# First products of a stage made in the pauses of the stage ahead, at five seams, and one expert split beside the ternary layer

## The chip, the cores and the metric

The kernel runs on one core of one Trainium2 chip. The metric is the device time of one execution in microseconds, median of several runs; lower is better. The core has a matrix engine (TensorE, PE), a vector engine (VectorE, DVE), a scalar engine (ScalarE, ACT), GpSimd (POOL) and a synchronising engine (SyncE, SP) that issues most transfers. TensorE writes into PSUM, which has eight banks.

## The reference

Two blocks, each an attention followed by a feed-forward part, every part with a residual and a layer norm. Input: 2 x 1024 rows of 512.

```
x = layernorm(x + L0_attn(x))   # q, k, v products, rope, causal softmax, 32 query heads on 8 key heads, wo
x = layernorm(x + L0_ffn(x))    # layer norm, absmax rounding, ternary w_fc (512 -> 2048), exact gelu,
                                # layer norm, absmax rounding, ternary w_proj (2048 -> 512)
x = layernorm(x + L1_attn(x))   # features elu(x Wqk + b), silu(x Wv + b), silu(x Wu + b); kv = k^T v;
                                # out = layernorm(q kv) * u; out Wo + b    (16 heads of 32, linear attention)
x = layernorm(x + L1_ffn(x))    # 16 routed experts (512 -> 2 x 352 -> 512, top 2) and a shared one twice as wide
```

The experts' weights come as 32-bit floats. A product of 32-bit accuracy is made from half-precision parts: each operand is split into a high and a low half, and high x high, high x low and low x high are added up (12 matmuls for a 128 x 512 result over 512 columns).

## The kernel before

The rows are worked in tiles of 128. The program is a row of stages, each a `Phase` with its own buffers, semaphores and PSUM banks and a block in which each engine has its own instruction list; between two stages all engines meet at a barrier. The stages, by the span's time: layer 0 of the attention (0 to 346, first batch) and layer 1 (346 to 666, second batch), both by `attention_layer`; `ternary_ffn` (to 907); `linear_features` ("lin", the feature stage, to 1099); `linear_output_and_route` ("out", to 1211); `dispatch` ("disp", to 1318.5); the routed experts; the shared half and the sum. The order within an engine's list is written out by hand: `unrolled` takes a table of (delay, function) pairs and calls, step by step, each function for the tile that is due; the attention's order comes from a planner that the change doesn't touch.

*The attention's two layers.* A tile is turned (`transpose_parts`, L164), multiplied with q, k and v weights (`products`, L156, 12 matmuls each), rotated on VectorE (L772, L777) and GpSimd (L892), and turned again (L550). At the end of a layer each of eight row tiles has its ending: VectorE normalises, ScalarE (L730) and GpSimd (L942) make the halves, TensorE turns them (event "x") and multiplies with wo (event "w", L156); VectorE adds and normalises (L868, L209, L226). Layer 1 also prepares two "early rows" for the ternary layer: `early_rows` on VectorE, `early_root` on GpSimd.

*The ternary layer.* Per tile 32 matmuls `fc` (L1084, four banks), gelu on ScalarE (L1106), mean and spread, normalisation (ScalarE L1138), maximum (VectorE L990), clip (L996), high half (ScalarE L1133), low half (VectorE L1194), a transpose by DMA into `hT`, 32 matmuls `proj` (L1094), residual (L1199) and norm. Between the normalisation and the next maximum one row block of the feature stage's weights is split (`next_high` L1144, `next_low` L1210).

*The feature stage.* Per tile three banks of `weighed` (L1337, 12 matmuls each) with a `biased` matmul each (L1341), exponential and tanh on ScalarE (L1434, L1439), VectorE (L1485 and on), then `kv` (L1411, L1417). Beside it `ExpertSplit` works on the weights of 14 experts, seven pieces each, 98 in all: load (SyncE), high half (ScalarE L1312), low half (VectorE L1317), store, in a ring of six; `spread` gives each tile's step its share of them.

*Output and routing, dispatch.* `q` (L1602) multiplies features with kv; near the end a tile is turned (L164), ScalarE evacuates it (L1671), `logit` follows (L1631). `dispatch` begins with `SharedHalf.gate_up` (24 matmuls of 128 x 352 a tile, L156), turns (L1782) and `down` (L1791), with the routing's sums and scatters between.

## Time and profile before

| | us |
|---|---|
| runs (3), lowest, median, highest | 1738.38, 1739.52, 1745.71 |
| profiled execution, its own time | 1740.19 |
| its span | 1738.4 |
| TensorE busy | 1585.8 (91%) |
| VectorE busy | 1176.6 (68%) |
| ScalarE busy | 933.9 (54%) |
| GpSimd busy | 576.3 (33%) |
| mean granted clock of TensorE | 0.973 |

The span runs from the first to the last instruction. Busy times of engines overlap. The granted clock is a share of 2.4 GHz: 0.5 is the lower level, 1.2 GHz, and a value between them is a mean over a stretch with both. Matmuls are pipelined, so a group's busy time counts and not the sum of single ones.

### The profile page before, as it was taken

How to read it: one execution, taken by the hardware profiler on the slowest of the kernel's cores; microseconds unless marked ns; L12 is line 12 of the kernel's file. 1: busy time of each engine (PE TensorE's matmuls, PEld its weight loads, DVE VectorE, ACT ScalarE, POOL GpSimd, SP SyncE). 2: the span in 40 equal slices, each digit the busy share in tenths (PEclk: the TensorE clock that was granted, in tenths of full speed). 3: DMA queues.
4: the chain of work that ended last, by engine and by line, in shares of the span. 5: the costliest groups of instructions: out<-in, count | busy, mean ns of one | idle time of the engine just before them, and what ended most of it. 6: DMA issues, size and time to landing. Idle time of an engine off the chain costs nothing. (4 is left out here: it accounts for less than half of the span.)

```text
span 1738.4 us, 33564 instructions
## 1 busy us (share of the span) xinstructions
PE 1585.8 (91%) x12554; PEld 803.7 (46%) x12554; DVE 1176.6 (68%) x2074; ACT 933.9 (54%) x1641; POOL 576.3 (33%) x583
## 2 busy tenths in 40 slices
PE   6899999889999997999978999687898899999997
PEld 3533333364333342444434444454555556666564
DVE  4599998468999955899857777895723243333387
ACT  5756777345677754767736665476223333333332
POOL 4556575161000021223321111595271111111265
PEclk9999999899999998999999999798999999999999
DMA  7323332000000002655638999551151764456344
GB/s 248 137 39 56 76 68 48 2 1 2 14 2 2 2 2 63 125 109 110 106 73 315 353 334 363 179 182 61 55 101 51 276 226 167 154 179 219 105 126 134
DMA packets 177842, 211.42 MB, mean 122 GB/s; under 512 B 114203, under 2 KB 117625, under 8 KB 175505
## 3 DMA queue, kind: packets, MB, share of 16 engines
q1 hardware_dynamic: 170336, 188.54, 36.3%
q0 software_dynamic: 7344, 20.73, 4.4%
q8 instruction: 101, 1.65, 0.4%
q14 instruction: 61, 0.49, 0.1%
HBM read 193.33 MB, written 56.40 MB: 144 GB/s over the span
## 5 line engine op out<-in xcount | busy, mean ns | idle before, releaser
L717 ACT ACTIVATE layer_scratch<-layer_banks 128x512 f32<-128x512 f32 x576 | 312.5, 596 | 128.7 <-PE layer_banks L609 127.2
L828 DVE TENSOR_REDUCE layer_mx<-layer_banks 128x2 f32<-128x1024 f32 (+3 forms) x304 | 339.2, 1156 | 24.0 <-PE layer_banks L587 20.6
L2218 PE MATMUL sparse_ps_g<-wgate,sparse_xT 128*128 128x352 f16 x1128 | 185.5, 315 | 1.6 <-DVE sparse_xT L2296 1.6
L624 PE MATMUL layer_banks<-layer_scratch,V 128*32 128x256 f32 x2304 | 174.5, 389 | 0.8 <-ACT layer_scratch L725 0.8
L1337 PE MATMUL lin_ps_z<-arena,early 128*128 128x512 f16 x576 | 134.5, 384 | 6.8 <-PEq L1044 3.5
L2218 PEld LDWEIGHTS sparse_ps_g<-wgate,sparse_xT 128*128 128x128 f16 x1128 | 108.9, 98 | 63.1 <-DVE sparse_xT L2296 2.0
L2302 DVE SCALAR_TENSOR_TENSOR sparse_hid<-sparse_th,sparse_ps_g 128x352 f32<-128x352 f32 x47 | 24.5, 521 | 155.8 <-ACT sparse_th L2263 155.8
L2329 POOL DMA_INDIRECT xg<-x_d,token x45 | 42.6, 947 | 252.5 <-PE sparse_ps_x L2208 252.5
L1094 PE MATMUL ffn_ps_y<-wprojT,ffn_hT 128*128 128x512 f16 x512 | 116.1, 386 | 8.0 <-DMA ffn_hT<-ffn_h 8.0
L1084 PE MATMUL ffn_ps_fc<-wfcT,early 128*128 128x512 f16 x512 | 114.7, 383 | 5.7 <-PEq L950 3.4
L587 PE MATMUL layer_banks<-KT,arena 64*128 64x512 f16 (+3 forms) x768 | 113.8, 330 | 6.5 <-DVE layer_mx L828 6.3
L609 PE MATMUL layer_banks<-arena,KT 64*128 64x256 f16 x1152 | 111.9, 273 | 6.1 <-ACT layer_scratch L717 4.3
L2250 PE MATMUL sparse_ps_y<-wdown,sparse_hT 128*128 128x512 f16 (+1 forms) x423 | 100.6, 383 | 10.4 <-ACT sparse_hT L2276 9.1
L1317 DVE SCALAR_TENSOR_TENSOR lin_sp_parts<-lin_sp_raw,lin_sp_parts 128x704 f16<-128x704 f32 (+2 forms) x98 | 78.6, 840 | 36.6 <-ACT lin_sp_parts L1312 36.5
L1312 ACT ACTIVATE lin_sp_parts<-lin_sp_raw 128x704 f16<-128x704 f32 (+2 forms) x98 | 67.3, 718 | 55.8 <-DMA lin_sp_raw<-in_L_ffn_w_gate_up_dram 40.2
L1337 PEld LDWEIGHTS lin_ps_z<-arena,early 128*128 128x128 f16 x576 | 53.6, 99 | 73.2 <-issue 13.5
L220 POOL TENSOR_TENSOR ffn_lnr_rstd<-ffn_lnr_var,minus_half 128x1 f32<-128x1 f32 x16 | 36.7, 2297 | 141.7 <-DVE ffn_lnr_var L215 141.7
L1094 PEld LDWEIGHTS ffn_ps_y<-wprojT,ffn_hT 128*128 128x128 f16 x512 | 50.6, 99 | 71.4 <-DVE ffn_r L1199 5.5
L1084 PEld LDWEIGHTS ffn_ps_fc<-wfcT,early 128*128 128x128 f16 x512 | 50.2, 98 | 68.5 <-issue 6.4
L942 POOL TENSOR_TENSOR layer_turned_rows<-O,layer_turned_rows 128x512 f16<-128x512 f32 x16 | 18.5, 1158 | 186.7 <-ACT layer_turned_rows L730 186.7
L624 PEld LDWEIGHTS layer_banks<-layer_scratch,V 128*32 128x32 f32 x2304 | 49.6, 108 | 63.8 <-issue 35.1
L609 PEld LDWEIGHTS layer_banks<-arena,KT 64*128 64x128 f16 x1152 | 39.0, 94 | 86.1 <-issue 42.0
(305 smaller groups left out, 3129.4 us busy)
## 6 DMA issues: line engine op xcount, KB each, us to landing
wgate<-gate_d SPq DMA_DIRECT2D x47, 1408.0 KB
wdown<-down_d SPq DMA_DIRECT2D x47, 768.0 KB
lin_sp_raw<-in_L_ffn_w_gate_up_dram SPq DMA_DIRECT2D x56, 352.0 KB, 5.0
gate_d<-lin_sp_parts SPq DMA_DIRECT2D x56, 352.0 KB, 4.8
y_d<-y SPq DMA_DIRECT2D x47, 256.0 KB
down_d<-lin_sp_parts SPq DMA_DIRECT2D x42, 256.0 KB, 4.7
lin_sp_raw<-in_L_ffn_w_down_dram SPq DMA_DIRECT2D x28, 256.0 KB, 5.3
wfcT<-in_L_ffn_w_fc_dram SPq DMA_DIRECT2D x8, 512.0 KB, 7.6
```

The source lines that it names most:

```text
L587: last = pe.matmul(slots[par][:, h, :], QT[s, pair + h, qt * P:(qt + 1) * P], KT[s, (pair + h) // 2, c * 512:c * 512 + n], start=not diago ...
L609: last = pe.matmul(ps_t[:, (2 * g + par) % 3, i, :], KT[s, j, kt * P:(kt + 1) * P], QT[s, 2 * j:2 * j + 2, qt * P:(qt + 1) * P], start=kt ...
L624: last = pe.matmul(ps_o[32 * jj:32 * jj + 32, 256 * half:256 * half + 256], V[:, kt, 4 * jg + jj, :], prob[(2 * q + jj // 2) % 4][:, half, ...
L717: act.activation(prob[g % 4][:, par, :, :], ps_t[:, (2 * g + par) % 3, :, :], ACT.Exp, scale=HD ** -0.5).then_inc(exp_done, 1)
L828: dve.tensor_reduce(mx[x % 2][:, c, :, at:at + per], ps_s[:, 2 * (r % 2):2 * (r % 2) + 2, 0:per * n].rearrange("p e (h k) -> p e h k", k=n ...
L1084: last = pe.matmul(ps_fc[n][:, :], xT[u][:, part, k, :], m.wfcT[:, k, n * D:(n + 1) * D], start=(k == 0 and part == 0), stop=(k == KC - 1 ...
L1094: last = pe.matmul(ps_y[u][:, :], hT[u][:, part, k, :], m.wprojT[:, k, :], start=(k == 0 and part == 0), stop=(k == NK - 1 and part == 1))
L1312: act.activation(self.part(i, 0), self.raw[u][0:rows, 0:width], ACT.Copy, scale=WS).then_inc(self.hi_done, 1)
L1317: dve.scalar_tensor_tensor(self.part(i, 1), self.raw[i % self.ring][0:rows, 0:width], WS, self.part(i, 0), ALU.mult, ALU.subtract).then_in ...
L1337: pe.matmul(out, xT[:, a, k, :], m.w1[:, i, b, k, :], start=(k == 0 and n == 0), stop=False)
L2218: last = pe.matmul(ps_g[u][n][rows, :], xT[u][:, a, k, rows], w, start=(k == 0 and i == 0), stop=(k == KC - 1 and i == 2), skip_group_chec ...
L2250: last = pe.matmul(ps_y[u][rows, :], hT[u][0:size, a, k, rows], w, start=(k == 0 and i == 0), stop=(k == 2 and i == 2), skip_group_check=L ...
```

## The change

All stages share one PSUM tensor of eight banks, `m.banks`, so that a result can stay in its bank over a barrier. At five seams the stage ahead makes products of the next stage's first tiles.

- Layer 0 to layer 1: the 12 q matmuls of tile 0 (128 x 512) ahead of the turning of the last tile, the 12 k matmuls (128 x 128) behind the last wo. Layer 1 makes only v for tile 0.
- Layer 1 to the ternary layer: 8 fc matmuls of tile 0 ahead of the last turning, 16 behind the last wo; 8 remain.
- Ternary layer to feature stage: 24 `weighed` matmuls ahead of the last `proj`, 12 behind it; only the three `biased` remain for tile 0.
- Feature stage to output: 18 query matmuls of tiles 0 and 1 ahead of the last `kv`; 6 remain.
- Output to dispatch: 42 gate-up matmuls of tiles 0 and 1 ahead of the last four logits; 6 remain.

In layer 1 `early_rows` takes its statistics a step earlier, its two normalisations in steps 5 and 6 instead of both in step 6, and stands behind `qlo` instead of ahead of `first_maxima`; `early_root` moves a step earlier. One expert's seven pieces move from the feature stage (91 left) to the ternary layer, one in every second step, with a ring of three.

```diff
+        def next_projection(pe, at, size):
+            out = banks[:, 4:6, :].rearrange("p n c -> p (n c)")[:, at:at + size]
+            products(pe, out, lambda k: xT[0][:, 0, k, :], lambda k: xT[0][:, 1, k, :],
+                     lambda k: m.wqkv_h[:, k, at:at + size], lambda k: m.wqkv_l[:, k, at:at + size], KC)
+        def next_layer(pe, n):
+            ternary_products(pe, m, m.banks[:, 4 + n, :], xT[0], n)
...
                 if kind == "x":
                     t, = a
+                    if t == TB - 1:
+                        pe.wait_ge(exp_done, 4 * len(QUADS))
+                        pe.wait_ge(early_in[0], 16)
+                        if ternary:
+                            next_projection(pe, 0, D)
+                        else:
+                            next_layer(pe, 0)
                     pe.wait_ge(ol_done, t + 1)
...
                              lambda k: m.wo_h[:, k, :], lambda k: m.wo_l[:, k, :], KC).then_inc(y_done, 1)
+                    if t == TB - 1 and ternary:
+                        next_projection(pe, D, KV)
+                    elif t == TB - 1:
+                        next_layer(pe, 1)
+                        next_layer(pe, 2)
...
             def early_rows(t, u):
-                    if t == 4:
+                    if t == 3:
                         early_ln.statistics(dve, m.X[:, n, :][:, None, :], n, n)
-                    if t == 6:
+                    if t == 5 + n:
                         early_ln.normalize(dve, early_x[n][:, :], m.X[:, n, :], n, n)
...
                 def proj(t):
+                    if t == NT - 1:
+                        pe.wait_ge(gelu_done, NT * NB)
+                        pe.wait_ge(xt_in[0], 16 * (NT // 2))
+                        pe.wait_ge(w1l_done, NT)
+                        for i in range(2):
+                            weighed(pe, m, m.banks[:, 4 + i, :], i, xT[0])
...
+                    if t == NT - 1:
+                        weighed(pe, m, m.banks[:, 6, :], 2, xT[0])
...
-                                      (4, of_layer(h_norm)), (1, of_layer(next_high))])
+                                      (4, of_layer(h_norm)), (1, of_layer(next_high)),
+                                      (5, split.every_second(split.high, act))])
...
-                                      (1, of_layer(x_norm)), (1, of_layer(next_low))])
+                                      (1, of_layer(x_norm)), (1, of_layer(next_low)), (5, split.every_second(split.low, dve))])
...
-        split = ExpertSplit(f, m, d, 6, 0, LIN_EXPERTS, 0)
+        split = ExpertSplit(f, m, d, 6, FFN_EXPERTS, LIN_EXPERTS - FFN_EXPERTS, 0)
...
                 def kv(t):
+                    if t == NT - 1:
+                        pe.wait_ge(xt_evac, NT - AHEAD)
+                        pe.wait_ge(kvl_done, 4)
+                        for n in range(2):
+                            queries(pe, m, n, range(KC - 1))
                     pe.wait_ge(k_done, t + 1)
...
+                def shared(t):
+                    if t == NT - 4:
+                        pe.wait_ge(split.lo_done, split.count)
+                        pe.wait_ge(n1_done, NT)
+                        shared_gate_up(pe, m, 0, 0, range(KC))
+                    if t == NT - 3:
+                        shared_gate_up(pe, m, 0, 1, range(KC - 1))
+                    if t == NT - 2:
+                        pe.wait_ge(wt_evac, NT)
+                        shared_gate_up(pe, m, 1, 0, range(KC))
+                    if t == NT - 1:
+                        shared_gate_up(pe, m, 1, 1, range(KC - 1))
-                unrolled(NT, [(3, wt), (0, q), (8, xt), (9, logit), (4, wo), (2, router)])
+                unrolled(NT, [(3, wt), (0, q), (8, xt), (9, shared), (9, logit), (4, wo), (2, router)])
```

VectorE in the ternary layer, before: the low half of a weight row block (into `arena`), then the maximum of the gelu rows `ffn_hn` and their clip.

```order
L1210 SCALAR_TENSOR_TENSOR arena<-ffn_raw,arena 128x512
L990 TENSOR_REDUCE ffn_qh_g<-ffn_hn 128x1
L993 TENSOR_SCALAR ffn_qh_limit<-ffn_qh_g 128x1 x2
L996 TENSOR_SCALAR ffn_hn<-ffn_hn,ffn_qh_limit 128x2048
L1177 TENSOR_REDUCE ffn_whole<-ffn_sums 128x1
```

The same place now, in every second tile:

```order
L1264 SCALAR_TENSOR_TENSOR arena<-ffn_raw,arena 128x512
L1372 SCALAR_TENSOR_TENSOR ffn_sp_parts<-ffn_sp_raw,ffn_sp_parts 128x704
L1033 TENSOR_REDUCE ffn_qh_g<-ffn_hn 128x1
L1036 TENSOR_SCALAR ffn_qh_limit<-ffn_qh_g 128x1 x2
L1039 TENSOR_SCALAR ffn_hn<-ffn_hn,ffn_qh_limit 128x2048
```

A piece's low half stands between the weight row block's low half and the maximum.

TensorE at the seam from the ternary layer to the feature stage, before: the last three `proj` in one row (96 matmuls), the two branches at the barrier, then the feature stage's first products.

```order
L1094 MATMUL ffn_ps_y<-wprojT,ffn_hT 128x512 x96
L1044 UNCONDITIONAL_BRANCH
L1379 UNCONDITIONAL_BRANCH
L1337 MATMUL lin_ps_z<-arena,early 128x512 x36
L1341 MATMUL lin_ps_z<-bias,ones_row 128x512 x3
```

And now:

```order
L1145 MATMUL banks<-wprojT,ffn_hT 128x512 x64
L1401 MATMUL banks<-arena,early 128x512 x24
L1145 MATMUL banks<-wprojT,ffn_hT 128x512 x32
L1401 MATMUL banks<-arena,early 128x512 x12
L1088 UNCONDITIONAL_BRANCH
L1452 UNCONDITIONAL_BRANCH
L1405 MATMUL banks<-bias,ones_row 128x512 x3
```

All 36 products stand ahead of the barrier, 24 of them between the last two `proj`.

TensorE at the seam from output to dispatch, before: turning the last tile, two tiles' logits, the barrier, the gate-up products of two tiles.

```order
L164 MATMUL out_ps_x<-ident,out_x 128x128 x8
L1631 MATMUL out_ps_l<-out_gT,xT 128x16 x32
L1571 UNCONDITIONAL_BRANCH
L2077 UNCONDITIONAL_BRANCH
L156 MATMUL disp_ps_g<-arena,xT 128x352 x48
```

And now, from the same turning on:

```order
L170 MATMUL banks<-ident,out_x 128x128 x8
L1840 MATMUL banks<-arena,xT 128x352 x12
L1703 MATMUL banks<-out_gT,xT 128x16 x16
L1840 MATMUL banks<-arena,xT 128x352 x9
L1703 MATMUL banks<-out_gT,xT 128x16 x16
L1647 UNCONDITIONAL_BRANCH
L2173 UNCONDITIONAL_BRANCH
L1840 MATMUL banks<-arena,xT 128x352 x6
```

21 of the 42 products that moved stand here ahead of the last two logits, 21 more ahead of the two logits before.

## Rows read from the trace of the kernel before

**Rows 1.** Windows: span, busy us (count) by engine, PEclk, DMA share, GB/s

```profile
340.00:360.00 20.00, 15.01 (x123) 8.66 (x122) 9.38 (x23) 2.86 (x6) 7.62 (x12) 0.86 0.01 2
...
666.20:906.60 240.40, 226.55 (x1024) 100.81 (x1024) 196.13 (x382) 157.92 (x225) 61.92 (x62) 0.98 0.55 105
...
906.60:1098.70 192.10, 177.70 (x928) 87.33 (x928) 141.38 (x202) 112.01 (x186) 34.22 (x32) 0.96 0.90 324
```

**Rows 2.** Timeline (start, us, engine, operation, [idle before, releaser]), layer 0 end

```profile
335.92 1.04 PE L164 MATMUL layer_banks<-ident,layer_turned_rows 128*128 128x128 f16 x8 [2.77 <-POOL layer_turned_rows L942]
...
337.74 0.61 PE L156 MATMUL layer_banks<-wo_h,layer_turned_rows 128*128 128x512 f16 x1 [0.79 <-DVE layer_turned_rows L864]
...
342.67 0.69 DVE L868 SCALAR_TENSOR_TENSOR layer_r<-layer_banks,X 128x512 f32<-128x512 f32 x1 [4.53 <-PE layer_banks L156]
```

**Rows 3.** Timeline, layer 1's start

```profile
346.03 0.58 PE L156 MATMUL layer_banks<-wqkv_h,early 128*128 128x512 f16 x1 [3.40 <-PEq L950]
...
348.24 0.09 DVE L809 MEMSET layer_top<- 128x16 uint32 x2
...
351.63 0.82 DVE L772 TENSOR_TENSOR layer_scratch<-layer_banks,consts 128x640 f32<-128x640 f32 x1 [3.31 <-PE layer_banks L156]
```

**Rows 4.** Timeline, early rows in layer 1, its end, ternary layer start

```profile
385.42 1.81 PE L550 MATMUL layer_banks<-ident,layer_scratch 128*128 128x128 f16 x24 [2.64 <-DVE layer_scratch L783]
...
663.16 0.69 DVE L868 SCALAR_TENSOR_TENSOR layer_r<-layer_banks,X 128x512 f32<-128x512 f32 x1 [4.88 <-PE layer_banks L156]
...
672.99 1.28 ACT L1106 ACT_TABLE_LOAD   x1
```

**Rows 5.** Timeline, the ternary layer's loop in the middle and near its end

```profile
750.27 2.28 DVE L990 TENSOR_REDUCE ffn_qh_g<-ffn_hn 128x1 f32<-128x2048 f32 x1
...
750.93 7.07 PE L1094 MATMUL ffn_ps_y<-wprojT,ffn_hT 128*128 128x512 f16 x32
...
763.93 2.28 DVE L990 TENSOR_REDUCE ffn_qh_g<-ffn_hn 128x1 f32<-128x2048 f32 x1
...
764.75 1.46 PE L1094 MATMUL ffn_ps_y<-wprojT,ffn_hT 128*128 128x512 f16 x6
...
870.38 2.29 DVE L990 TENSOR_REDUCE ffn_qh_g<-ffn_hn 128x1 f32<-128x2048 f32 x1 [2.90 <-ACT ffn_hn L1138]
...
872.95 1.35 DVE L996 TENSOR_SCALAR ffn_hn<-ffn_hn,ffn_qh_limit 128x2048 f32<-128x2048 f32 x1
...
876.13 1.90 ACT L1133 ACTIVATE ffn_h<-ffn_hn 128x2048 f16<-128x2048 f32 x1
```

**Rows 6.** Timeline, the seam to the feature stage

```profile
894.71 8.75 PE L1094 MATMUL ffn_ps_y<-wprojT,ffn_hT 128*128 128x512 f16 x32 [5.03 <-DMA ffn_hT<-ffn_h]
...
916.86 0.80 PE L1341 MATMUL lin_ps_z<-bias,ones_row 33*128 33x512 f16 x3 [2.01 <-DVE bias L1470]
```

**Rows 7.** Feature stage: window, groups (count | busy, mean ns | idle), timeline

```profile
940.00:960.00 20.00, 20.00 (x111) 10.11 (x111) 16.02 (x23) 12.86 (x22) 4.32 (x4) 1.00 0.98 360
...
L1317 DVE SCALAR_TENSOR_TENSOR lin_sp_parts<-lin_sp_raw,lin_sp_parts 128x704 f16<-128x704 f32 (+2 forms) x97 | 77.9, 841 | 36.0 <-ACT lin_sp_parts L1312 35.8
L1312 ACT ACTIVATE lin_sp_parts<-lin_sp_raw 128x704 f16<-128x704 f32 (+2 forms) x98 | 67.3, 718 | 55.8 <-DMA lin_sp_raw<-in_L_ffn_w_gate_up_dram 40.2 <-DMA lin_sp_raw<-in_L_ffn_w_down_dram 15.6
...
1089.94 0.57 ACT L1434 ACTIVATE lin_e<-lin_ps_z 128x512 f32<-128x512 f32 x1
...
1093.25 2.08 PE L1411 MATMUL lin_ps_kv<-lin_tanh,lin_relu 128*128 128x128 f32 x8 [6.21 <-POOL lin_relu L1530]
```

**Rows 8.** Timeline, the two last seams

```profile
1099.95 0.70 DVE L209 BATCH_NORM_STATS2 out_lnq_stats<-out_ps_q 128x6 f32<-128x512 f32 x1 [0.24 <-PE out_ps_q L1602]
...
1205.77 1.01 PE L164 MATMUL out_ps_x<-ident,out_x 128*128 128x128 f16 x8 [2.08 <-ACT xT L1671]
...
1211.24 9.59 PE L156 MATMUL disp_ps_g<-arena,xT 128*128 128x352 f16 x48 [0.53 <-PEq L1571]
...
1221.00 3.74 PE L156 MATMUL disp_ps_g<-arena,xT 128*128 128x352 f16 x24
```

134 lines of the change are left out of this document (82 added, 52 removed).

## The prediction

> **What bounds the kernel now.** The window table by stage comes first [rows 1]. The reader is to see that the ternary layer and the feature stage are the two stages of which the change moves work across a border, that the first has TensorE busy for 226.6 of 240.4 us and the second for 177.7 of 192.1 with its DMA engines at 0.90, and that the twenty microseconds around the first seam ran at a mean granted clock of 0.86: part of that window stood at 1.2 GHz, the lower of the two levels, the rest at 2.4. The timelines at the seams come second. They show the same thing five times: TensorE waits 2.8 to 6 us for another engine's last conversion, what it then does runs at the lower level, a barrier of about 3.4 us follows, and the new stage begins with products whose operands were there long before. The steady parts come last, since one piece of the change (an expert's seven pieces in the ternary layer) is not a seam but work in a loop.
>
> The profiled execution took 1740.19 us, the span 1738.4; the median of the three runs, 1739.52, is 0.7 below the profiled one. I make the sum against the profiled execution and take 0.7 off at the end. A measurement of this kernel can tell about 0.5% (8.7 us) from no change.
>
> **Seam 1, ahead of the barrier: -2.4 (+2.1 to -2.7).** TensorE waits 2.77 us for GpSimd's low half, turns the last tile in 1.04 us and makes the twelve products of wo in 4.93 us, from 337.74 to VectorE's addition at 342.67 [rows 2]. That is 0.41 us each, whereas 32 products of the same shape (128x512) take 7.07 us, 0.22 each, in the ternary layer [rows 5]. The change puts twelve such products in the wait: 2.65 us at the fast level, so they just fit, and TensorE does not rest before the transposes. Then wo takes 2.65 (-2.3) and the transposes about half (-0.4, an estimate); 0.3 is given back if the filling ends late. If the clock falls all the same, twelve products at 0.41 take 4.9 in a wait of 2.77: +2.1. The twelve small k products behind wo lie beside VectorE's normalisation, which starts at 342.67 and has some 3 us to the next stage's first product at 346.03 [rows 3].
>
> The Trainium skill, "TensorE: Matmul & The Clock Gate", Part 1, says that activity releases the throttle and idling puts it back. The rows agree (0.41 behind the wait, 0.22 in the unbroken stretch); by that rule a filled wait gives back its clock, here the -2.4 above.
>
> **Seam 1, behind the barrier: -2.5 (-1.5 to -3.3).** The first rotation on VectorE (L772) comes at 351.63 after waiting 3.31 us for TensorE, which began at 346.03 [rows 3]. With q and k there already, the rotation waits for VectorE's own clearing, which ends at 348.33 [rows 3], and TensorE has only twelve v products of 128 columns. The gain is 351.63 - 348.33 = 3.3. Against it, TensorE then rests before tile 1, whose first eight products may cost 0.19 more each: 1.5. I take 0.8 of it.
>
> **The early rows of layer 1: +0.5 (-1 to +2).** Statistics, root and normalisation of the two early tiles move by a step, and the normalisations from one step to two. Before, TensorE lost 2.64 us there to VectorE's conversion L783 and then ran slow [rows 4]. The same VectorE work now stands in two steps, behind that conversion and ahead of the next rotation: two small delays for one large.
>
> **Seam 2: -2.3 (-2.9 to +4).** The same tail: VectorE waits 4.88 us for wo [rows 4]. Eight products in the wait (1.8 us) keep the clock: -2.3 - 0.4. The sixteen behind wo need 3.5 us, VectorE's normalisation from 663.16 on some 3.0, as at seam 1: +0.4. At the lower level they would take 6.6: +3.6. Behind the barrier I count nothing: the first gelu waits for ScalarE's conversions, which come by DMA, and its table, loaded at 672.99 [rows 4], not for products.
>
> **The first expert in the ternary layer: +3.9 (+0.3 to +6.5).** In the steady stretch TensorE is busy throughout, a projection every 13.82 us (750.93, 764.75), and the other engines have a loop of their own: VectorE's maximum of the gelu rows (L990), clip, high half, squares, roots, normalisation, one weight row's high and low half, the next maximum; it comes every 13.66 us (750.27, 763.93) [rows 5]. Each piece puts its high half (0.72 us on ScalarE) and low half (0.84 on VectorE) [rows 7] between that weight row's low half and the maximum; ScalarE's share lies beside the weight row's low half, so the loop grows by some 0.9. It has seven pieces in seven tiles: 6.4. What hides it? TensorE's work hides the loop in the middle, but not at the end: the last projection waits 5.03 us for the loop's transposed rows [rows 6], so the loop's lateness arrives there in full, less the loop's own slack in the last two tiles. There the high half of ScalarE begins at 876.13, behind gelu, while the clip that it needs, begun at 872.95, was done at 874.30 [rows 5]: 1.8 of slack, and for the tile before I take 0.7, an estimate. 6.4 - 2.5 = 3.9. The lower end is a loop with slack for all pieces, the upper one without any. The seven loads and stores (SyncE's queue, two steps ahead of their use and two behind) stand beside transposes that are issued 7 us later; I count nothing for them.
>
> **Seam 3: -1.5 (-1.9 to +4.8).** 24 products (5.3 us) fill that wait of 5.03, and the last projection falls from 8.75 to 7.07 us [rows 5, 6]: -1.7 + 0.2. The twelve behind it lie beside VectorE's normalisation. Behind the barrier the biases' product at 916.86 waits for VectorE's bias rows, loaded by DMA after the barrier [rows 6], so the 36 products that are gone there were hidden: 0.
>
> **The feature stage with 91 pieces for 98: -7 (-3.5 to -8.8).** TensorE is busy for 20.00 of 20 us in the middle, DMA at 0.98 and 360 GB/s, and ScalarE waited 55.8 us in all for pieces [rows 7]. Pieces come every 1.82 us (98 from the first loads, some 5 us into the stage, to the last exponential at 1089.94, so in some 178 us). TensorE's 177.7 us over 16 tiles are 11.1 a tile [rows 1], in which the DMA brings 6.1 pieces; 98 over 16 tiles ask for 6.13, 91 for 5.69. Before, the pieces therefore fell behind, and the last kv product waited 6.21 us, after which it ran at the low level for 2.08 [rows 7]. Now supply keeps up. The start gains 1.2 (two pieces for three ahead of the first exponential, one piece being 0.72 and its wait). At the end nine pieces for ten stand ahead of the last exponential, and the exponential before it comes earlier. If all of the wait goes: 6.2 + 1.2 for the start + 1.4 for the last kv and k products at full clock (half of 2.08 and of what follows) = 8.8, which is the floor that TensorE sets. If only the pieces fewer at either end count, with the same waits: 1.2 + 1.3 + 1.0 = 3.5. I take 7, since four pieces in flight at a time still need some 1.5 us each behind the last but one tile.
>
> **Seams 4 and 5: -0.25 and -1.3 (-3 to +6).** The 18 query products fit what is left of the wait at 1093.25 [rows 7]; behind the barrier VectorE's statistics waited 0.24 for TensorE [rows 8], and that goes. At seam 5, 42 products of 128x352 at 0.156 (24 in 3.74 us) [rows 8] are 6.5 us ahead of four logits, in a tail whose longest wait is 2.08 [rows 8]; the transposes behind them run at full clock, at half of 1.01. Followed row by row, some 4.3 us of the 6.5 lie in waits or are won by the clock, and the end comes 2.2 later (an estimate). Behind the barrier TensorE had 9.59 us of gate-up products, and the third tile's began at 1221.00, 9.8 after the start [rows 8]. Now it has six, so the chain over ScalarE, VectorE and GpSimd sets the third tile, some 4.7 after the start, with a rested TensorE that costs about 1.5: -3.5. Sum -1.3.
>
> **Sum.** -2.4 - 2.5 + 0.5 - 2.3 + 3.9 - 1.5 - 7 - 0.25 - 1.3 = -12.9. 1740.2 - 12.9 = 1727.3, and 0.7 less for the median: **1726.6 us**.
>
> **The rivals.** (a) The seven pieces are hidden, since the loop has more slack than the two tiles show: 1723.0. For it: VectorE was busy 196 of 240 us [rows 1]. Against it: the maximum follows the weight row without a pause. Chance 0.14. (b) The feature stage gives the lower bound of 3.5, pieces still setting the last exponential: 1730.1. For it: four in flight; chance 0.14. (c) The stage follows its bytes: seven pieces at 1.82 are 12.7 us, and the total 1720.9. Against it: TensorE was busy throughout, and its floor is 8.8. Chance 0.04.
>
> The Trainium skill, "DMA: Bandwidth & Descriptors", Specifications, gives a core about 358 GB/s from HBM, and the trace shows 360 there. By that figure alone the seven pieces (4.3 MB read and written) would be some 12 us, an estimate that is rival (c).
>
> (d) Slower than before: the clock does not stay up in the waits, and the moved products run at 0.41 (0.31 for 352 columns). Then seam 1 gives +2.1, seam 2 +0.5 + 3.6, seam 3 +4.8 and seam 5's 42 products take 13 us for 6.5, so +5.2 for -1.3. With -2, +0.5, +3.9, -7 and -0.25 for the rest that is +11.4: 1751. It decides from some 0.3 us a product on. For it: TensorE ran at 0.41 behind each wait. Against it: it ran at the fast level up to the wait, and now goes on without one. Chance 0.04. (e) The products were hidden anyway and the seams give nothing, with only the pieces left: +3.9 - 7 = -3.1, 1736.4; for it speaks that seams 2 and 3 give nothing behind the barrier by my own reading. Chance 0.08.
>
> **How the numbers follow.** The forecast has 0.56, with 1722 to 1731 as its own range. (a), (c) and (b) lie within or beside that; (d) and the lower half of (e) are left out. Range 1718 to 1736. Faster by over 0.5% means below 1730.8: the forecast but for 0.04 of it, (a), (c) and half of (b): 0.77. Same: (e), the other half of (b) and 0.04: 0.19. Slower: 0.04.
>
> **What would show it.** In the profile after: wo at the two layers' ends in about 2.7 us and no granted clock below 0.95 in the windows there; the first rotation 2.4 after the barrier; the first maximum behind each piece 0.9 later than its neighbours'; the last transposed rows of the ternary layer some 4 us later against TensorE's last fc; the last kv product of the feature stage waiting under 2 us; the logits' tail 2 us longer and the third gate-up 5 us sooner. The prediction is wrong if ht of tile 15 comes no later (a), if the last exponential still trails by 5 us (b), or if products in the waits take 0.4 us each (d).

## The result

Before 1739.34 us (median of 15 runs, 1731.31 to 1745.71), after **1728.31** (15 runs, 1723.16 to 1733.33): ratio 0.9933, 95% interval 0.9921 to 0.9945, so 11.0 us less, and more than the 0.5% that can be told from no change. The forecast was 1726.6 within 1718 to 1736. The profiled execution after took 1729.09, its span 1727.3.

The stages show where the 11.1 us between the two profiled executions lie. A stage begins with TensorE's first row behind its barrier (the feature stage with ScalarE's); a "tail" runs from the layer's last row sums to that point. The last column is what the sum forecast.

| stage, us | before | after | difference | forecast |
|---|---|---|---|---|
| layer 0 without its tail | 332.52 | 334.98 | +2.46 | 0 |
| tail of layer 0 | 13.51 | 10.97 | -2.54 | -2.4 |
| layer 1 without its tail | 306.64 | 305.76 | -0.88 | -2.5 + 0.5 |
| tail of layer 1 | 13.85 | 11.32 | -2.53 | -2.3 |
| ternary layer | 240.38 | 243.81 | +3.43 | +3.9 - 1.5 |
| feature stage | 192.11 | 187.17 | -4.94 | -7 |
| mixing and logits | 112.23 | 112.47 | +0.24 | -0.25 + 2.2 |
| dispatch | 107.27 | 104.21 | -3.06 | -3.5 |
| routed experts, combination | 419.89 | 416.61 | -3.28 | 0 |

The first and the last line hold no changed work. In the kernels below, which have the same work there, layer 0 takes 330.1 to 333.9 us and the two last stages 414 to 422. The changed stages give -10.28 in this profile.

**The seams' tails.** Timeline of after, the two layers' ends (start, duration, engine, operation, count, [idle before, and what ended it]):

```profile
338.38 0.62 PE L170 MATMUL banks<-ident,layer_turned_rows 128*128 128x128 f16 x8 [0.18 <-POOL layer_turned_rows L976]
...
339.78 0.39 PE L162 MATMUL banks<-wo_h,layer_turned_rows 128*128 128x512 f16 x1 [0.79 <-DVE layer_turned_rows L898]
...
342.58 0.69 DVE L902 SCALAR_TENSOR_TENSOR layer_r<-banks,X 128x512 f32<-128x512 f32 x1 [2.40 <-PE banks L162]
...
652.18 1.89 PE L1017 MATMUL banks<-wfcT,early 128*128 128x512 f16 x8
655.11 0.62 PE L170 MATMUL banks<-ident,layer_turned_rows 128*128 128x128 f16 x8 [1.04 <-POOL layer_turned_rows L976]
...
659.32 0.69 DVE L902 SCALAR_TENSOR_TENSOR layer_r<-banks,X 128x512 f32<-128x512 f32 x1 [2.40 <-PE banks L162]
```

At the first seam the wait of 2.77 [rows 2] has shrunk to 0.18: the twelve q products stand in it. The transposes take 0.62 for 1.04, and from wo's first row to VectorE's addition 2.80 us pass where there were 4.93; VectorE waits 2.40 for 4.53 there, and 2.40 for 4.88 at the second layer's end [rows 2, 4].

**The start of layer 1.** Timeline of after, then its windows (busy us and count by engine, granted clock, DMA share, GB/s):

```profile
345.95 0.22 PE L162 MATMUL banks<-wqkv_h,early 128*128 128x128 f16 x1 [2.73 <-PEq L984]
...
347.85 1.03 PE L170 MATMUL banks<-ident,early 128*128 128x128 f16 x8 [1.07 <-POOL early L920]
...
348.30 0.82 DVE L806 TENSOR_TENSOR layer_scratch<-banks,consts 128x640 f32<-128x640 f32 x1
...
349.97 0.61 PE L162 MATMUL banks<-wqkv_h,early 128*128 128x512 f16 x1 [1.09 <-DVE layer_scratch L811]
...
356.24 0.82 DVE L806 TENSOR_TENSOR layer_scratch<-banks,consts 128x640 f32<-128x640 f32 x1 [2.14 <-PE banks L162]
```
```profile
346.00:356.00 10.00, 7.84 (x56) 4.41 (x57) 4.81 (x13) 2.50 (x5) 6.21 (x10) 0.66 0.01 3
356.00:366.00 10.00, 8.52 (x106) 6.37 (x104) 7.37 (x18) 3.94 (x7) 5.44 (x10) 1.00 0.00 0
```

The first rotation (L806) comes 2.35 us after the stage's start at 345.95, where it came 5.60 after [rows 3]. But the second comes at 10.29 (before: 11.42) and the third at 17.99 (before: 17.54): the start's 3.25 us are gone by the third tile. TensorE rests 2.73 us at the barrier and, with only v products to make, stands idle twice more for 1.1 us; the granted clock of these ten microseconds is 0.66, and the second projection's first products follow one another every 0.43 us, not every 0.215.

**The ternary layer.** Timeline of after, VectorE around one piece, then TensorE at the layer's end; the line behind them is VectorE's in the kernel before, at the same place of a tile:

```profile
762.84 2.28 DVE L1033 TENSOR_REDUCE ffn_qh_g<-ffn_hn 128x1 f32<-128x2048 f32 x1
...
775.90 0.69 DVE L1264 SCALAR_TENSOR_TENSOR arena<-ffn_raw,arena 128x512 f16<-128x512 f32 x1 [0.71 <-ACT arena L1197]
776.58 0.89 DVE L1372 SCALAR_TENSOR_TENSOR ffn_sp_parts<-ffn_sp_raw,ffn_sp_parts 128x704 f16<-128x704 f32 x1
777.39 2.28 DVE L1033 TENSOR_REDUCE ffn_qh_g<-ffn_hn 128x1 f32<-128x2048 f32 x1
```
```profile
882.57 8.75 PE L1145 MATMUL banks<-wprojT,ffn_hT 128*128 128x512 f16 x32 [4.23 <-DMA ffn_hT<-ffn_h]
891.15 5.34 PE L1401 MATMUL banks<-arena,early 128*128 128x512 f16 x24
```
```profile
749.66 0.69 DVE L1210 SCALAR_TENSOR_TENSOR arena<-ffn_raw,arena 128x512 f16<-128x512 f32 x1 [0.71 <-ACT arena L1144]
```

From maximum to maximum 14.55 us pass with a piece between, 0.89 more than the 13.66 before [rows 5]. In both kernels VectorE is idle for 0.71 us ahead of the weight row's low half, waiting for ScalarE. At the end it is now the last projection but one that waits, 4.23 us, and then takes 8.75; the last one, which waited 5.03 before [rows 6], follows the 24 moved products without a pause.

**The feature stage and the last seams.** Group of the pieces on ScalarE in after (count | busy, mean ns | idle before), then timelines of after:

```profile
L1367 ACT ACTIVATE lin_sp_parts<-lin_sp_raw 128x704 f16<-128x704 f32 (+2 forms) x91 | 60.9, 715 | 33.6 <-DMA lin_sp_raw<-in_L_ffn_w_gate_up_dram 20.9 <-DMA lin_sp_raw<-in_L_ffn_w_down_dram 12.6
```
```profile
916.85 1.43 PE L1405 MATMUL banks<-bias,ones_row 33*128 33x512 f16 x3 [10.85 <-DVE bias L1546]
...
1088.25 2.08 PE L1487 MATMUL banks<-lin_tanh,lin_relu 128*128 128x128 f32 x8 [2.40 <-POOL lin_relu L1606]
```
```profile
1206.48 1.06 PE L1840 MATMUL banks<-arena,xT 128*128 128x352 f16 x6 [0.53 <-PEq L1647]
...
1210.67 5.42 PE L1840 MATMUL banks<-arena,xT 128*128 128x352 f16 x24
```

The biases' product still waits for VectorE's bias rows and begins 10.0 us after the stage's start, as before [rows 6]: the 36 products that are gone ahead of it were hidden there. ScalarE waits 33.6 us for pieces where it waited 55.8, and the last kv product waits 2.40 for 6.21, still at the lower level in 2.08 us [rows 7]. The third tile's gate-up (L1840) begins 4.2 us after the dispatch stage's start, where it began 9.8 after [rows 8].

### The profile page after: what moved, and what is told of

It reads as the page before. It is cut to its first block and busy times, and to the rows that moved or that the text cites. A ratio compares the mean times of both kernels' runs of the same rounds, so it can differ in the third digit from the quotient of the medians.

```text
span 1727.3 us, 33567 instructions
## 1 busy us (share of the span) xinstructions
PE 1576.4 (91%) x12554; PEld 799.2 (46%) x12554; DVE 1172.6 (68%) x2074; ACT 931.7 (54%) x1641; POOL 578.2 (33%) x583
## 5 line engine op out<-in xcount | busy, mean ns | idle before, releaser
L751 ACT ACTIVATE layer_scratch<-banks 128x512 f32<-128x512 f32 x576 | 312.5, 595 | 129.5 <-PE banks L631 127.9
L862 DVE TENSOR_REDUCE layer_mx<-banks 128x2 f32<-128x1024 f32 (+3 forms) x304 | 339.2, 1155 | 24.1 <-PE banks L609 20.8
L2314 PE MATMUL banks<-wgate,sparse_xT 128*128 128x352 f16 x1128 | 184.4, 313 | 1.6 <-DVE sparse_xT L2392 1.6
L646 PE MATMUL banks<-layer_scratch,V 128*32 128x256 f32 x2304 | 174.5, 389 | 0.8 <-ACT layer_scratch L759 0.8
L1401 PE MATMUL banks<-arena,early 128*128 128x512 f16 x576 | 134.6, 384 | 0.3 <-DVE lin_relu L1561 0.3
L2398 DVE SCALAR_TENSOR_TENSOR sparse_hid<-sparse_th,banks 128x352 f32<-128x352 f32 x47 | 24.5, 521 | 154.0 <-ACT sparse_th L2359 154.0
L1840 PE MATMUL banks<-arena,xT 128*128 128x352 f16 x768 | 121.8, 315 | 2.0 <-PEq L2262 1.4
L1017 PE MATMUL banks<-wfcT,early 128*128 128x512 f16 x512 | 115.3, 383 | 7.3 <-ACT ffn_h L1159 6.5
L1145 PE MATMUL banks<-wprojT,ffn_hT 128*128 128x512 f16 x512 | 114.8, 383 | 7.3 <-DMA ffn_hT<-ffn_h 7.1
L609 PE MATMUL banks<-KT,arena 64*128 64x512 f16 (+3 forms) x768 | 113.8, 330 | 6.7 <-DVE layer_mx L862 6.6
L631 PE MATMUL banks<-arena,KT 64*128 64x256 f16 x1152 | 111.9, 273 | 6.1 <-ACT layer_scratch L751 4.3
L1840 PEld LDWEIGHTS banks<-arena,xT 128*128 128x128 f16 x768 | 74.3, 99 | 39.5 <-issue 2.5
```

The lines of the kernel that those rows point to most:

```text
L609: last = pe.matmul(slots[par][:, h, :], QT[s, pair + h, qt * P:(qt + 1) * P], KT[s, (pair + h) // 2, c * 512:c * 512 + n], start=not diago ...
L631: last = pe.matmul(ps_t[:, (2 * g + par) % 3, i, :], KT[s, j, kt * P:(kt + 1) * P], QT[s, 2 * j:2 * j + 2, qt * P:(qt + 1) * P], start=kt ...
L646: last = pe.matmul(ps_o[32 * jj:32 * jj + 32, 256 * half:256 * half + 256], V[:, kt, 4 * jg + jj, :], prob[(2 * q + jj // 2) % 4][:, half, ...
L751: act.activation(prob[g % 4][:, par, :, :], ps_t[:, (2 * g + par) % 3, :, :], ACT.Exp, scale=HD ** -0.5).then_inc(exp_done, 1)
L862: dve.tensor_reduce(mx[x % 2][:, c, :, at:at + per], ps_s[:, 2 * (r % 2):2 * (r % 2) + 2, 0:per * n].rearrange("p e (h k) -> p e h k", k=n ...
L1017: last = pe.matmul(out, xT[:, part, k, :], m.wfcT[:, k, n * D:(n + 1) * D], start=(k == 0 and part == 0), stop=(k == KC - 1 and part == 1))
```

## Experiments

Each kernel is the changed one with the edit shown. One execution has only its time; several have a median, their count and, as ratio to the kernel before, an interval.

### Is the gain the clock's, and must the products stand in the wait?

The same products at the first three seams, all moved behind the layer's last product:

```diff
                         pe.wait_ge(early_in[0], 16)
-                        if ternary:
-                            next_projection(pe, 0, D)
-                        else:
-                            next_layer(pe, 0)
...
                     if t == TB - 1 and ternary:
+                        next_projection(pe, 0, D)
                         next_projection(pe, D, KV)
                     elif t == TB - 1:
+                        next_layer(pe, 0)
...
-                        for i in range(2):
-                            weighed(pe, m, m.banks[:, 4 + i, :], i, xT[0])
...
                     if t == NT - 1:
-                        weighed(pe, m, m.banks[:, 6, :], 2, xT[0])
+                        for i in range(3):
+                            weighed(pe, m, m.banks[:, 4 + i, :], i, xT[0])
```

> The changed kernel with the products that stood in TensorE's waits at the first three seams put behind the last product of the stage (behind the last wo, behind the last projection); the same products are made ahead of the barrier, only the waits are empty again. Theory: an empty wait lets the clock fall, so wo takes 4.9 us again in place of 2.6, and the last projection 8.7 in place of 7.1; the tail of layer 0 goes from 11.0 us to 13.5 or more, that of layer 1 from 11.3 to 16 or more since 24 products then stand behind wo. Rival: the gain came from the products' leaving the next stage alone, the clock is set by something else, and wo stays at 2.6 us.

Measured: 1737.93 (one execution). Layer 0's tail takes 12.60 us, layer 1's 16.12, the ternary layer 249.16. Timeline and windows of this kernel at the two layers' ends:

```profile
333.83 0.61 PE L170 MATMUL banks<-ident,layer_turned_rows 128*128 128x128 f16 x8 [2.97 <-POOL layer_turned_rows L974]
...
653.27 0.61 PE L162 MATMUL banks<-wo_h,layer_turned_rows 128*128 128x512 f16 x1 [0.79 <-DVE layer_turned_rows L896]
...
658.61 0.69 DVE L900 SCALAR_TENSOR_TENSOR layer_r<-banks,X 128x512 f32<-128x512 f32 x1 [4.94 <-PE banks L162]
```
```profile
334.00:340.00 6.00, 5.21 (x25) 2.21 (x23) 1.84 (x3) 0.00 (x0) 0.00 (x0) 0.72 0.00 0
652.00:660.00 8.00, 7.21 (x24) 2.74 (x23) 2.51 (x4) 0.00 (x0) 0.00 (x0) 0.58 0.01 2
```

Windows of the change at the same places:

```profile
336.00:342.00 6.00, 5.04 (x30) 2.28 (x28) 1.57 (x4) 0.63 (x1) 1.16 (x1) 1.00 0.00 0
654.00:660.00 6.00, 4.17 (x26) 2.05 (x26) 1.83 (x3) 0.00 (x0) 1.05 (x1) 1.00 0.01 3
```

With the wait open again (2.97), wo runs at the lower level at layer 1's end, 5.34 us from its first row to the addition, and VectorE waits 4.94 for it, as it did before the change (4.88 [rows 4]); the granted clock is 0.58 there and 1.00 in the change. The same products, moved by a few lines, cost 1.6, 4.8 and 5.4 us more at the three seams, 11.8 together, while the time is 9.6 above the change's. At layer 1's end 2.5 of the 4.8 are wo's clock (5.34 against the 2.81 that it takes in the change); the rest is the eight products that stand in the tail now and in the wait there.

### The start of layer 1

The early rows of layer 1 as before: the root and the statistics a step later, both normalisations in one step and ahead of the maxima.

```diff
-                    if t == 3:
+                    if t == 4:
...
-                    if t == 5 + n:
+                    if t == 6:
...
-            unrolled(TB, [(1, of(xevac)), (1, of(weights_low)), (2, of(rope)), (3, of(evac)), (2, of(first_maxima)), (2, of(qlo)), (0, of(early_rows)),
+            unrolled(TB, [(1, of(xevac)), (1, of(weights_low)), (2, of(rope)), (3, of(evac)), (0, of(early_rows)), (2, of(first_maxima)), (2, of(qlo)),
...
-                if not first and t == 4:
+                if not first and t == 5:
```

> The changed kernel with the early rows of layer 1 in the order of before (statistics in step 4, both normalisations in step 6, ahead of the first maxima). In the changed kernel layer 1 takes 305.8 us from its start to the last sum of the softmax; it was 306.6. By the theory of the prediction the new order costs some 0.5, so this takes 305.3. Rival one: the start's gain of 3.3 us was really there and the new order ate it, so this takes 303 to 304. Rival two: the start's gain was lost to the slow products of tile 1 and the new order is a gain, so this takes 306.5 or more.

Measured: 1724.85 (one execution), layer 1 306.59. The first rotation is at 2.35 here too, the second at 10.95 and the third at 16.80; the layer as a whole is as long as before (306.64). From the second rotation to the third it is 5.85 us here and 7.70 in the change, where VectorE makes the early rows' statistics in between: the new order delays the third tile by 1.85, but the layer does not end later for it. In the ten kernels with the new order and no other edit there it takes 305.56 to 306.54, in this one 306.59, so the new order gains some 0.5 us, little more than the spread. It is rival two that fits: most of the start's gain is lost at the second tile, whatever the early rows do.

So TensorE's pauses were filled, behind the first v products (second call) and behind the transposes that follow (first call), on top of the order of ScalarE's row that is tried further down:

```diff
+                if b and t == ahead:
+                    filled(pe)
+
+            def filled(pe):
+                for k in range(4):
+                    pe.matmul(banks[:, 0, :], xT[1][:, 0, k, :], m.wqkv_h[:, k, 0:D], start=(k == 0), stop=(k == 3))
...
                 last.then_inc(proj_done, 1)
+                if b and t == 0:
+                    filled(pe)
```

> The former kernel plus eight products of 128x512 that nothing uses, four in each of TensorE's two first waits of the second layer (1.07 and 1.09 us in the changed kernel), written to a bank that the next projection overwrites. Theory (the start's gain of 3.25 us shrank to 1.1 at the second rotation because TensorE rested there and ran the second projection at 0.43 us a product): the granted clock of the second layer's first ten microseconds rises from 0.66 to over 0.9, the second rotation comes some 8.3 us after the stage's start in place of 10.29, and the layer is 1 to 2 us shorter, 304 to 305. Rival one (the clock falls in spite of it): the fill costs its own 1.7 at the lower level, the second rotation comes at 10.3 to 12 and the layer takes 306 to 307. Rival two (VectorE's own chain sets the tiles that follow): the second rotation is earlier, but the third comes 17 to 18 after the start as before and the layer keeps its 305.5 to 306.

Measured: 1725.62 (4 executions), 0.9916 (0.9899 to 0.9934). Timeline and windows of this kernel, whose layer 1 starts at 343.69:

```profile
344.36 1.03 PE L543 MATMUL banks<-wqkv_h,early 128*128 128x512 f16 x4
345.59 0.62 PE L170 MATMUL banks<-ident,early 128*128 128x128 f16 x8 [0.20 <-POOL early L928]
346.04 1.03 PE L543 MATMUL banks<-wqkv_h,early 128*128 128x512 f16 x4
347.72 0.39 PE L162 MATMUL banks<-wqkv_h,early 128*128 128x512 f16 x1 [0.65 <-DVE layer_scratch L819]
```
```profile
340.00:350.00 10.00, 6.42 (x53) 3.50 (x52) 5.78 (x17) 1.54 (x4) 3.81 (x6) 1.00 0.01 3
346.00:356.00 10.00, 9.12 (x87) 5.65 (x84) 5.23 (x9) 2.81 (x6) 7.42 (x14) 1.00 0.00 0
```

The eight useless products keep the granted clock at 1.00; the second rotation comes at 8.17 (10.29 in the change), and the lead is still there at the eighth: 49.92 against 51.94. That shows what the start lost. Of these 2.0 us layer 1 keeps 0.4 to 1.3 (305.19): what absorbs the rest between the projections and the layer's end was not traced. The total shows nothing of it: the order of ScalarE's row alone had 1722.59 on the same chip, and the two intervals overlap; in the profiled execution here the feature stage took 188.6.

The kernel with the products behind the wait shows that the two later pauses do not lower the clock by themselves. Timeline and windows of that kernel at the same place:

```profile
342.83 0.22 PE L162 MATMUL banks<-wqkv_h,early 128*128 128x128 f16 x1 [0.30 <-PEq L982]
...
346.87 0.39 PE L162 MATMUL banks<-wqkv_h,early 128*128 128x512 f16 x1 [1.52 <-DVE layer_scratch L809]
```
```profile
342.83:352.83 10.00, 7.17 (x86) 5.28 (x87) 6.51 (x17) 2.83 (x6) 6.35 (x11) 1.00 0.01 3
```

Its 24 products fill the time up to the barrier, so TensorE rests 0.30 us there for 2.73 in the change; the two pauses behind it are open (1.06 and 1.52), and the granted clock is 1.00 all the same. The second rotation comes at 8.17 as in the filled start, and the layer takes 305.23. The low clock of the change thus needed both the rest at the barrier and the pauses behind it; to fill either was enough here.

### The first expert: what it costs and what it gives

```diff
-FFN_EXPERTS = 1
+FFN_EXPERTS = 0
```

> The changed kernel with all 14 experts in the feature stage again (98 pieces, none in the ternary layer); the five seams stay. Theory: the seven pieces lengthen VectorE's and ScalarE's loop of the ternary layer and all but 2.5 us of that arrives at the last projection, so the ternary layer falls from 243.8 us to about 239, and the feature stage rises from 187.2 to about 192; the whole time stays within 1 us of the changed kernel's. Rival: the pieces were hidden in the ternary layer (243.8 stays, what it lost comes from the products put ahead of the last projection), and the time rises by 5.

Measured: 1726.51 (4 executions), 0.9936 (0.9915 to 0.9956). The ternary layer takes 237.85, the feature stage with all 98 pieces 192.59. So the seam at the ternary layer's end gives 240.38 - 237.85 = 2.5, the seven pieces cost 243.81 - 237.85 = 6.0 and save 192.6 - 187.2 = 5.4: moving the expert is worth nothing in the change, and the whole gain is that of the seams.

```diff
-                                      (4, of_layer(h_norm)), (1, of_layer(next_high)),
-                                      (5, split.every_second(split.high, act))])
+                                      (1, of_layer(next_high)), (5, split.every_second(split.high, act)),
+                                      (4, of_layer(h_norm))])
```

> The changed kernel with ScalarE's two high halves of each step in the ternary layer (the weight rows' and the expert piece's) ahead of the normalisation of the gelu rows, where ScalarE waits about 2 us for GpSimd, in place of behind it. Theory: the loop of the ternary layer is a chain over four engines in which the high and low halves stand between the normalisation and the maximum; out of that place the loop is shorter by about 1.2 us a tile and the pieces cost nothing, so the ternary layer falls from 243.8 to 240 or less and the time by about 4. Rival: the halves wait for their loads there or push the normalisation back by as much, and the layer stays at 243.8 or gets longer.

Measured: 1720.07 (4 executions), 0.9901 (0.9878 to 0.9924); the ternary layer takes 236.51 with its seven pieces. Timeline of this kernel, VectorE and ScalarE around a piece, then TensorE at the layer's end:

```profile
768.48 0.68 DVE L1264 SCALAR_TENSOR_TENSOR arena<-ffn_raw,arena 128x512 f16<-128x512 f32 x1
769.08 0.88 DVE L1372 SCALAR_TENSOR_TENSOR ffn_sp_parts<-ffn_sp_raw,ffn_sp_parts 128x704 f16<-128x704 f32 x1
769.89 2.28 DVE L1033 TENSOR_REDUCE ffn_qh_g<-ffn_hn 128x1 f32<-128x2048 f32 x1
...
782.75 2.28 DVE L1033 TENSOR_REDUCE ffn_qh_g<-ffn_hn 128x1 f32<-128x2048 f32 x1
```
```profile
765.00 0.77 ACT L1367 ACTIVATE ffn_sp_parts<-ffn_sp_raw 128x704 f16<-128x704 f32 x1
766.63 2.10 ACT L1191 ACTIVATE ffn_hn<-ffn_h,ffn_shift,ffn_rstd 128x2048 f32<-128x2048 f32 x1 [0.85 <-POOL ffn_shift L1281]
```
```profile
875.28 7.07 PE L1145 MATMUL banks<-wprojT,ffn_hT 128*128 128x512 f16 x32 [0.29 <-DMA ffn_hT<-ffn_h]
```

ScalarE makes the halves while it would wait for GpSimd's shift anyway, and VectorE's low halves stand ahead of the normalised rows that its maximum needs. The idle 0.71 in front of L1264 is gone. From the maximum before (at 756.21) to the one behind the piece it is 13.68 us, and to the next, without a piece, 12.86, where the change had 14.55 and 13.66. TensorE's projection period of 13.82 [rows 5] is the longer of the two again, and the last projection but one waits 0.29.

Run again beside the change itself on one chip:

> The changed kernel with one thing else: on ScalarE the high halves of weight rows and pieces stand ahead of the normalisation of the gelu rows in each step. Theory (a piece cost the loop its place and not its work: VectorE waited for ScalarE's half behind that normalisation, so the loop grew by 0.9 per piece): the ternary layer takes 236 to 237 us with its seven pieces, 7.3 less than in the change, and the time is 7 lower than the change's beside it, 1719 to 1722. Rival (the run of 1720.07 was a lucky one, untouched stages having varied by 2 to 5): the two times differ by less than 3.

Measured: 1722.59 (5 executions), 0.9898 (0.9884 to 0.9911), ternary layer 237.77. The change beside it:

> The changed kernel once more, to stand beside the next one on the same chip. Both theories of the ternary layer expect 1726 to 1730 us, a ternary layer of 243.5 to 244.5 with the last but one projection behind a wait of some 4.2 us, and a feature stage of 184 to 187.

Measured: 1728.92 (6 executions), 0.9927 (0.9906 to 0.9947), ternary layer 244.14. The medians differ by 6.3, the ternary layers by 6.4; the two intervals only just overlap. The ternary layers leave no room for the rival of a lucky run. Is the order a gain without pieces too? The same two edits together:

> The seams stay and the expert stays in the feature stage (0 pieces in the ternary layer, 98 behind it), but ScalarE's high halves of the weight rows stand ahead of its normalisation of the gelu rows, as in the run of 1720.07 us. Theory (in the old order VectorE waited some 0.7 us in each tile for a weight row's half that ScalarE made behind its normalisation, so the order is a gain of its own): the ternary layer takes about 235 us against 237.85 with the old order, and the pieces' own price is the 236.51 with them less this, 1 to 2 us; with the feature stage at 192.6 the time is about 1724. Rival (the order matters only for where the pieces stand): the ternary layer takes 237.85 as before, the pieces are free in the new order, and the time is 1726.5.

Measured: 1726.13 (one execution), ternary layer 237.65, feature stage 192.27. The rival holds: without pieces the order gives 0.2, since TensorE sets the pace then, and with it the pieces are free (236.51 and 237.77 with seven).

### What holds the feature stage

On top of the new order, the pieces are spread so that fewer stand in the last step:

```diff
-            return self.count if t == tiles else max(0, t * self.count // tiles - later)
+            return max(0, t * self.count // tiles - later * (tiles - t) // tiles)
```

> The new order on ScalarE, and in the feature stage the pieces' delay behind the tiles shrinks evenly to nothing, so that the last tile has some 6 pieces in place of 9 ahead of its exponential; the work is the same. Theory (nine pieces in the last step, each with its wait, hold the last exponential): the last exponential starts 2 to 3 us earlier against the stage's start, the last kv product waits under 1 us, the stage falls from 184.3 to about 181.5, the time to about 1717.5. Rival (pieces come at the DMA's pace whatever step they stand in): they wait earlier instead, the feature stage stays at 184 to 187 and the time at 1720; if the earlier pieces then hold the exponentials of the middle it gets slower, to 1723.

Measured: 1721.75 (5 executions), 0.9881 (0.9853 to 0.9909); feature stage 185.09, against 184.06 to 188.61 in the eight profiles with 91 pieces and the old spread. The last kv product follows without its wait, but ScalarE waits 43.2 us for pieces instead of 33.6: they wait earlier. The time is the rival's; where it went is told below. Then fewer pieces (in the new order, a piece in each of fourteen tiles):

```diff
-FFN_EXPERTS = 1
+FFN_EXPERTS = 2
...
-            if t % 2 == 0 and t // 2 < self.count:
-                fn(eng, t // 2)
+            if t < self.count:
+                fn(eng, t)
```

> The new order on ScalarE, and two experts (14 pieces, one in each of fourteen tiles) beside the ternary layer, 84 pieces in the feature stage. Theory (in the new order VectorE has room, since it was busy 149 of 160 us with a piece in every second tile and TensorE bounds the stage at 13.66 us a tile): the ternary layer rises by at most 2 us over 236.51, the feature stage falls to its TensorE floor of some 181, the time is about 1718. Rival one (VectorE, some 0.42 us a tile busier, becomes the bound): each tile takes 0.4 longer, the last projection waits, the ternary layer takes 241 to 244 and the time is 1721 or more. Rival two (the feature stage is no longer held by pieces at 91): it stays at 184, and the time is 1720 to 1722.

Measured: 1722.51 (4 executions), 0.9890 (0.9861 to 0.9918); ternary layer 236.65, feature stage 184.46. VectorE carries fourteen pieces for nothing in the new order, and ScalarE's wait for pieces falls to 14.0, but the stage keeps its 184: rival two. With the even spread as well:

> Two experts beside the ternary layer, 84 pieces in the feature stage, whose delay behind the tiles shrinks evenly to nothing, so that the last tile has some 5 pieces in place of 9. Theory (with 91 pieces the even order gave nothing because pieces came at the DMA's pace; with 84 the supply has room, since ScalarE waited only 14.0 us for pieces against 33.6): the last kv product of the feature stage follows the one before it without the wait of 2.41, and the stage takes some 182.5 against 184.46, the time some 1720.5. Rival (TensorE's own work is the stage's floor): the stage stays within 0.5 of 184.5 and the time at 1722.5.

Measured: **1719.78** (4 executions, 1719.11 to 1722.14), 0.9885 (0.9871 to 0.9899); feature stage 184.21, the last kv product without a wait. Again the time is the rival's, and it looks as if some 184 us were TensorE's floor. The rows tell otherwise. The table divides the stage at two rows of TensorE (the biases' products, L1405): the last of the second tile and the last of the sixteenth.

| kernels, by pieces in the feature stage; us | stage's start to the second tile | from there to the sixteenth | from there to the stage's end |
|---|---|---|---|
| 98: before and two more | 24.3 to 25.1 | 153.1 to 154.0 | 13.9 to 14.4 |
| 91: eight profiles | 22.0 to 23.8 | 152.3 | 9.8 to 12.8 |
| 84 | 22.4 | 152.3 | 9.7 |
| 91, even spread | 25.4 | 152.6 | 7.1 |
| 84, even spread | 24.8 | 152.3 | 7.1 |

Timeline of ScalarE at the stage's start with 84 pieces, which begins at 899.18, then with 84 pieces and the even spread, which begins at 896.47:

```profile
910.32 0.60 ACT L1510 ACTIVATE lin_e<-banks 128x512 f32<-128x512 f32 x1
```
```profile
907.20 0.79 ACT L1367 ACTIVATE lin_sp_parts<-lin_sp_raw 128x704 f16<-128x704 f32 x1 [1.43 <-DMA lin_sp_raw<-in_L_ffn_w_gate_up_dram]
...
909.82 0.60 ACT L1510 ACTIVATE lin_e<-banks 128x512 f32<-128x512 f32 x1
```

The even spread does give what its theory promised at the end, 2.6 us. It loses 2.4 at the start (3.3 with 91 pieces, against the 22.1 of the kernel of 1720.07), because it also puts a third piece, for which ScalarE waits 1.43 us, ahead of the first exponential: 13.35 us after the start for 11.14. The start of the one and the end of the other would make 22.4 + 152.3 + 7.1 = 181.8, an estimate that no kernel here tried. Only the middle is at TensorE's floor in these runs: 152.3 us with 91 pieces and with 84, and TensorE busy in it for 140.00 of 140 us. The kernel with 84 pieces and the even spread is 8.5 us below the change and the fastest of the series, though not apart from 1720.07 and 1721.75.

### The last seam

```diff
-                unrolled(NT, [(3, wt), (0, q), (8, xt), (9, shared), (9, logit), (4, wo), (2, router)])
+                unrolled(NT, [(3, wt), (0, q), (8, xt), (9, logit), (4, wo), (2, router)])
...
-        half = SharedHalf(f, m, 1, lambda c, k, size: m.ws_d[0:size, c, k, :], 2)
+        half = SharedHalf(f, m, 1, lambda c, k, size: m.ws_d[0:size, c, k, :], 0)
```

> The changed kernel without its fifth seam alone: the 42 gate-up products go back behind the barrier. My theory (seam 5 gives 1.3: the tail of the logits 2.2 longer, the stage behind it 3.5 shorter): the stage of the logits falls from 112.47 to about 110.3 us, the dispatch stage rises from 104.21 to about 107.7, the third tile's gate-up begins 9.8 us after the stage's start in place of 4.2, and the time rises by some 1.3. Rival one (the tail takes all of it back): both stages' sum stays within 0.5 us of 216.7. Rival two (the dispatch stage's end is set by GpSimd's and DMA's chain and not by its gate-up): the third gate-up comes 5.6 later but the dispatch stage stays at 104.2, and the time falls by 2. The dispatch stage has varied by 3 us between kernels with the same work there, so the rows decide and not the total.

Measured: 1734.81 (one execution), logits 112.04, dispatch 115.98; some 5 to 9 us of the latter are a stall late in the stage, told of below. Timeline of this kernel at the seam:

```profile
1199.28 9.65 PE L1840 MATMUL banks<-arena,xT 128*128 128x352 f16 x48 [0.53 <-PEq L1647]
...
1209.10 3.74 PE L1840 MATMUL banks<-arena,xT 128*128 128x352 f16 x24
1212.68 2.11 PE L1887 MATMUL banks<-arena,disp_hT 128*128 128x512 f16 x9
```

From the tail's transposes that wait 1.38 us for ScalarE, in both kernels, to the dispatch stage's start 8.54 us pass here and 10.32 in the change: the 42 products cost 1.8. From that start to the first product of the shared down projection (L1887) it is 13.4 here and 9.4 in the change: 4.0 back. The lead is still there at TensorE's next long wait (4.5 us in every kernel), 32.1 us after the start in the change, 36.1 here and 36.0 in the kernel before; behind that wait the stage takes 71.3 to 74.6 in the profiles without a stall, 71.3 of them in the kernel before. So the rival that the dispatch stage ends at the same time without the seam falls by these rows; the two stages' times alone, 104.2 and 116.0 with its stall, could not show it. The seam is worth 2.2 in the change's profile, against the 1.3 of my theory. In the other kernels with the seam the first down product comes 7.8 to 10.7 after the start, since the third gate-up's 24 products take 3.74 to 6.38 us; the worth is then 0.9 to 3.8.

## Why the prediction was right, point by point

- **Ahead of the barriers: right.** -2.54 and -2.53 for -2.4 and -2.3, in the place and by the mechanism named: the wait filled, wo and the transposes at the higher level. At the first, 2.13 in wo and 0.42 in the transposes are the whole of it; the products themselves cost nothing in the wait. Rival (d), the clock low in spite of the filling, fell. The Trainium skill, "TensorE: Matmul & The Clock Gate", Part 1, says that idling puts the throttle back; the traces agree both ways, 1.00 in the filled tails and 0.66 at the start of layer 1, where TensorE rests three times. Rival (e), the seams giving nothing, fell too: without the expert's move they bring 1726.51. The opening's picture of five like seams does not fit the last, whose longest wait was 2.08 and whose barrier 0.53 [rows 8].
- **Start of layer 1: too large.** I had -2.5 + 0.5 and it gave -0.9, and -0.5 on average over ten profiles. The 3.25 at the first rotation came as worked out; the step that failed is "I take 0.8" of a bound of 1.5 for TensorE's rest. The second projection alone gave 2.1 back, as the filled start shows. Nor does a lead at the rotations reach the layer's end whole: with the clock held the layer is 1.4 shorter than before (305.19 for 306.64), not 3.25. The early rows were put at +0.5 and came out at -0.5 in the layer's time, by a single profile.
- **The expert in the ternary layer: mis-sized, 6.0 for 3.9.** The 0.9 a piece was right. The wait came at the last projection but one, not at the last, and is 4.23 - 0.30 = 3.9 longer there than without pieces; but that projection then runs at the lower level, 8.75 for 7.07, which the sum had only for the last. I charged a piece its duration and did not ask what stood around it: VectorE's 0.7 us of idle in each tile, in the trace of before too, was room for it in another order. So the expert's move, forecast at +3.9 - 7 = -3.1, gave nothing. Rival (a), pieces hidden, was wrong of the change and right of the order tried later.
- **The seam at its end: too small, -2.5 for -1.5.** Together with the former +3.4 for +2.4.
- **The feature stage: right in size, the floor too high.** -4.9 in this profile; by the mean of the eight profiles with 91 pieces (186.0) against the three with 98 (192.3) -6.3, for -7 within -3.5 to -8.8. By the table above some 1.8 of the 6.3 came at the start, 1.4 in the middle and 3.1 at the end. TensorE's floor was put at 8.8 less than 192.1, 183.3; the kernels with 84 pieces stop at 184.5 and 184.2, but their best parts add up to 181.8. Rival (c), the stage following its bytes down by 12.7 us, fell: the middle takes 152.3 with 91 pieces and with 84. Rival (b), only 3.5, is what the slowest of the eight profiles shows (188.61). "The last kv product waiting under 2 us" failed by 0.4: its wait goes only with the even spread.
- **Last seams: right in kind.** Tail +1.8 for +2.2, behind the barrier -4.0 for -3.5, together -2.2 for -1.3. The query products' 0.25 was not tried alone; the mixing stage without the last seam took 112.04 for 112.23 before.
- **The sum.** -12.9 was forecast, the changed stages gave -10.3 in the profile and the medians -11.0. That the sum fell so near is in part luck: the misses of 1.5 at layer 1's start, 2.1 at the pieces and 0.6 in the feature stage were in part paid by the two seams that gave 1 more each and by 0.4 in the tails.

## What to carry to other kernels

Work put into a wait ahead of a chain's last products pays twice, by its own time and by the clock of what follows; the same work behind those products took 11.8 us more at three seams. Where a seam's work is taken away from behind a barrier, look at what TensorE does next: the rest at the barrier and two pauses of a microsecond behind it cost the following tile two, and in two other kernels, which filled the one or the other, the clock stayed up. And a piece that is put into a full loop is priced by the wait beside which it lands, so read on the engine that hands over (here ScalarE, which idled ahead of a normalisation) in which order it is free before counting its duration.
